# Attention heads: score banks, maxima banks, and the way the row sums leave PSUM

## The reference

```python
B, S, D, H = (4, 512, 512, 16)
DH = D // H
b, s, d = x.shape            # here b = 1, s = 2048, d = 512
q = (x @ Wq.T + bq).reshape(b, s, h, dh)
k = (x @ Wk.T + bk).reshape(b, s, h, dh)
v = (x @ Wv.T + bv).reshape(b, s, h, dh)
q = q * jnp.cos(rot)
k = k * jnp.sin(rot)
scores = jnp.einsum('bshd,bthd->bhst', q, k) / np.sqrt(dh)
scores = scores * spiral_weight[None, :, None, None]
attn = jax.nn.softmax(scores, axis=-1)
out = jnp.einsum('bhst,bthd->bshd', attn, v).reshape(b, s, d)
```

## Time and profile before

| | |
|---|---|
| median of 3 runs | 5249.96 us (5248.42 to 5251.48) |
| the profiled execution's span | 5264.5 us |
| PE, busy share of the span | 4694.6 us, 89% |
| DVE, ACT, POOL busy | 2373.3, 1652.7, 1662.5 us |
| the attention heads' stage | 1283 to 2275 us of the span |

### The profile page before, as it was taken

The page is one execution under the profiler, slowest core; times in us unless marked ns, Lnnn a source line. Parts: engine busy times, 40 slices in busy tenths (PEclk is TensorE's granted clock), DMA queues, the critical chain, the costliest instruction groups (busy, mean ns, idle before and its releaser), DMA issues. The chain is left out here.

```text
span 5264.5 us, 65210 instructions
## 1 busy us (share of the span) xinstructions
PE 4694.6 (89%) x25716; PEld 2520.4 (48%) x25716; DVE 2373.3 (45%) x3161; ACT 1652.7 (31%) x2791; POOL 1662.5 (32%) x1050
## 2 busy tenths in 40 slices
PE   7357997899999999986999869999999989789996
PEld 3123443433333333244666536666666654456663
DVE  7863778366666666853222223333333331412222
ACT  5414553211555555733111122222222210221111
POOL 1010000101888888023555401111111110145553
PEclk9678998999999999997999979999999999889998
DMA  2000000100000000016889730000000022468887
GB/s 72 0 2 19 6 0 8 60 0 1 1 1 1 1 1 1 1 68 184 253 260 259 169 119 23 31 31 31 23 31 31 23 81 80 157 173 257 256 257 200
DMA packets 237579, 417.60 MB, mean 79 GB/s; under 512 B 31472, under 2 KB 119536, under 8 KB 237296
## 3 DMA queue, kind: packets, MB, share of 16 engines
q1 hardware_dynamic: 179952, 270.89, 15.3%
q0 software_dynamic: 57344, 142.64, 11.1%
HBM read 297.53 MB, written 115.93 MB: 79 GB/s over the span
## 5 line engine op out<-in xcount | busy, mean ns | idle before, releaser
L2296 PE MATMUL linb_pr_ps<-lin_z,linb_wt 128*128 128x512 f32 x1536 | 678.9, 595 | 17.0 <-POOL linb_slope_own L2266 17.0
L1467 ACT ACTIVATE attc_prob<-attc_ps 128x512 f32<-128x512 f32 x1024 | 549.0, 596 | 426.6 <-PE attc_ps L1380 376.2
L1343 POOL TENSOR_TENSOR attc_acc<-attc_acc,attc_prob 128x2048 f32<-128x2048 f32 x144 | 651.4, 4524 | 68.0 <-ACT attc_prob L1467 49.9
L1491 DVE TENSOR_REDUCE attc_peak<-attc_ps 128x2 f32<-128x1024 f32 x384 | 469.6, 1225 | 256.1 <-PE attc_ps L1388 256.1
L1380 PE MATMUL attc_ps<-att_q,att_k 32*128 32x512 f32 x2048 | 527.7, 613 | 0.0
L2296 PEld LDWEIGHTS linb_pr_ps<-lin_z,linb_wt 128*128 128x128 f32 x1536 | 286.7, 192 | 343.3 <-issue 325.8
L1388 PE MATMUL attc_ps<-att_k,att_q 32*128 32x512 f32 x1536 | 442.3, 652 | 3.2 <-DVE attc_tot L1514 3.2
L2273 POOL TENSOR_TENSOR linb_sq<-linb_osb 128x512 f32<-128x512 f32 x64 | 70.1, 1096 | 1041.0 <-ACT linb_osb L2399 1041.0
L2472 DVE SCALAR_TENSOR_TENSOR linb_gated<-linb_osb,linb_norm_w,linb_proj 128x512 f32<-128x512 f32 x64 | 93.3, 1458 | 669.1 <-ACT linb_osb L2399 669.1
L1401 PE MATMUL attc_ps<-attc_prob,att_v 128*32 128x256 f32 (+1 forms) x3472 | 317.7, 438 | 0.3 <-ACT attc_prob L1467 0.3
L1023 DVE TENSOR_TENSOR_SCAN ssmb_state<-ssmb_decay,ssmb_bu 128x2048 f32<-128x2048 f32 x64 | 279.7, 4409 | 79.0 <-ACT ssmb_decay L970 79.0
(11 more groups left out here) (443 smaller groups left out, 7539.6 us busy)
## 6 DMA issues: line engine op xcount, KB each, us to landing
moe1w_wgu<-in_L_ffn_gate_up_proj SPq DMA_DIRECT2D x32, 1536.0 KB
moe2w_wgu<-in_L_ffn_gate_up_proj SPq DMA_DIRECT2D x32, 1536.0 KB
moe1w_wd<-in_L_ffn_down_proj SPq DMA_DIRECT2D x32, 512.0 KB
gated_features<-linb_gated SPq DMA_DIRECT2D x64, 256.0 KB
moe2w_wd<-in_L_ffn_down_proj SPq DMA_DIRECT2D x32, 512.0 KB
linc_gt<-gated_features SPq DMA_DIRECT2D x7, 2048.0 KB, 8.2
linb_wt<-in_L_attn_b_qkv_w SPq DMA_DIRECT2D x16, 768.0 KB
residual_rows<-residual SPq DMA_DIRECT2D x8, 1024.0 KB, 4.3
```

The lines of the kernel that those rows point to most:

```text
L1343: pool.tensor_tensor(acc[:, n % 2, :, :], before, prob[:, U % NP, :, :], ALU.add).then_inc(pool_done, 2 if at == 1 else 1)
L1467: nc.scalar.activation(prob[:, U % NP, h, :], ps[:, n % 3 if at < 0 else at % 6, :], ACT.Exp).then_inc(exp_done, 1)
L1491: V.tensor_reduce(peak[:, w // TT % 2, i % QH, 2 * hp:2 * hp + 2, b], ps[:, bank:bank + 2, :], axis=AX.X, op=ALU.max).then_inc(mx_used, 1)
L2296: last = nc.tensor.matmul(pr_ps[:, use % 2, :], wt[:, b, kind, k, :], z[:, k, t * NB:(t + 1) * NB], start=(k == 0), stop=(k == DT - 1))
```

## The change

Scores in groups 0 to 2 get four banks (0 to 3) in place of three. The uses get single banks, three of them in turn (4 to 6): each head's maximum is a use of its own, with its own wait, its own semaphore increment and its own reduction on DVE, and a use waits for the use three before it. The sums leave PSUM by a copy on ACT into `tot` (two buffers, semaphore `z_out`), and DVE inverts them there in four pieces of 128 columns, one in each of the units 2 to 5 of a block, and multiplies in unit 6. The accumulator of a block becomes two, for units 0 to 6 and 7 to 13 (HALF = 7), in a ring of three; POOL makes 12 adds instead of 13 a block, and `sums` has four sources instead of three.

```diff
+        HALF = 7
         SUMMED = (14, 15)
         POOLED = [i for i in range(TT) if i not in SUMMED]
         prob = L.sb("prob", [P, NP, QH, NB])
-        acc = L.sb("acc", [P, 2, QH, NB])
-        tot = L.sb("tot", [P, NB])
+        acc = L.sb("acc", [P, 3, QH, NB])
+        tot = L.sb("tot", [P, 2, NB])
         o_raw = L.sb("o_raw", [P, 2, NB])
...
-            got = ["A", "B"] if f < DT - 1 else []
-            if U >= LAG:
-                done = (U - LAG) % TT
-                if done == TT - 1:
-                    got.append("F")
-            if w % TT == 2 and ((f < DT - 1 and w > TT) or (f > 0 and w == 2)):
-                got.append("R")
+            got = [("peak", h) for h in (2, 3, 0, 1)] if f < DT - 1 else []
+            if U >= LAG and (U - LAG) % TT == TT - 1:
+                got.append(("sums", 0))
+            if w % TT == 2 and ((f < DT - 1 and w > TT) or (0 < f < DT and w == 2)):
+                got.append(("rows", 0))
             return got
 
-        use_at, n_use = {}, 0
+        LAST_GROUP = (DT - 1) * UNITS
+        use_at, sums_upto, others_upto = {}, [0], [0]
         for U in range(ALL + LAG):
-            for kind in uses_of(U):
-                use_at[U, kind] = n_use
-                n_use += 1
-        LAST_GROUP = (DT - 1) * UNITS
-        USES_BEFORE = min(n for (U, kind), n in use_at.items() if U >= LAST_GROUP)
-
-        def use_banks(U, kind):
-            if U >= LAST_GROUP:
-                return 6
-            return 3 + 2 * (use_at[U, kind] % 2)
+            for use in uses_of(U):
+                use_at[U, use] = len(sums_upto) - 1
+                sums_upto.append(sums_upto[-1] + (use[0] == "sums"))
+                others_upto.append(others_upto[-1] + (use[0] != "sums"))
+        USES_BEFORE = min(n for (U, use), n in use_at.items() if U >= LAST_GROUP)
+
+        def use_bank(U, use):
+            return 6 if U >= LAST_GROUP else 4 + use_at[U, use] % 3
+
+        def use_count(U, use):
+
+            return others_upto[use_at[U, use] + 1]
 
         def rows_block(U):
             f, w = U // UNITS, U % UNITS
             return (f * TC + w // TT - 1) if w > TT else (f * TC - 1)
+
+        def accumulator(n, half):
+            return acc[:, (2 * n + half) % 3, :, :]
...
                 for at, i in enumerate(POOLED):
-                    if at == 0:
+                    if at % HALF == 0:
                         continue
                     U = n * TT + i
                     pool.wait_ge(exp_done, (U + 1) * QH)
                     if at == 1 and n >= 2:
                         pool.wait_ge(z_done, n - 1)
-                    if at >= 2:
+                    if at == HALF + 1 and n >= 1:
+                        pool.wait_ge(z_done, n)
+                    if at % HALF >= 2:
                         pool.wait_ge(pool_done, n * len(POOLED) + at)
-                    before = prob[:, (U - 1) % NP, :, :] if at == 1 else acc[:, n % 2, :, :]
-                    pool.tensor_tensor(acc[:, n % 2, :, :], before, prob[:, U % NP, :, :], ALU.add).then_inc(pool_done, 2 if at == 1 else 1)
+                    to = accumulator(n, at // HALF)
+                    before = prob[:, (U - 1) % NP, :, :] if at % HALF == 1 else to
+                    pool.tensor_tensor(to, before, prob[:, U % NP, :, :], ALU.add).then_inc(pool_done, 2 if at % HALF == 1 else 1)
...
-            def take(U, kind):
-                n = use_at[U, kind]
-                if U >= LAST_GROUP:
-                    pe.wait_ge(mx_used, n)
-                elif n >= 2:
-                    pe.wait_ge(mx_used, n - 1)
-                return use_banks(U, kind)
+            def take(U, use):
+                n = use_at[U, use]
+                before = n if U >= LAST_GROUP else max(n - 2, 0)
+                if others_upto[before]:
+                    pe.wait_ge(mx_used, others_upto[before])
+                if sums_upto[before]:
+                    pe.wait_ge(z_out, sums_upto[before])
+                return use_bank(U, use)
 
             def score_bank(n):
-                if n < QH * LAST_GROUP:
-                    if n >= 3:
-                        pe.wait_ge(exp_done, n - 2)
-                    return n % 3
                 at = n - QH * LAST_GROUP
-                if at < 3:
-                    pe.wait_ge(exp_done, n - 2)
-                elif at < 6:
-                    pe.wait_ge(mx_used, USES_BEFORE)
+                if at < 4:
+                    if n >= 4:
+                        pe.wait_ge(exp_done, n - 3)
+                    return n % 4
+                if at < 6:
+                    pe.wait_ge(mx_used, others_upto[USES_BEFORE])
+                    pe.wait_ge(z_out, sums_upto[USES_BEFORE])
...
-            def maxima(U, kind, heads):
+            def maxima(U, heads):
                 f, w = U // UNITS + 1, U % UNITS
                 i, b = w // TC, w % TC
-                bank = take(U, kind)
                 for h in heads:
+                    bank = take(U, ("peak", h))
                     own = slice(h * DH, (h + 1) * DH)
-                    last = nc.tensor.matmul(ps[:, bank + h % 2, :], q[own, f, i * P:(i + 1) * P], k[own, f, b * NB:(b + 1) * NB],
-                                            start=True, stop=True)
-                last.then_inc(mx_done, 1)
+                    nc.tensor.matmul(ps[:, bank, :], q[own, f, i * P:(i + 1) * P], k[own, f, b * NB:(b + 1) * NB],
+                                     start=True, stop=True).then_inc(mx_done, 1)
...
-                sources = [prob[:, (n - 1) % NP, :, :], prob[:, n % NP, :, :], acc[:, n // TT % 2, :, :]]
+                sources = [prob[:, (n - 1) % NP, :, :], prob[:, n % NP, :, :], accumulator(n // TT, 0), accumulator(n // TT, 1)]
...
-                    maxima(U, "A", (2, 3))
+                    maxima(U, (2, 3))
                     if U >= LAG and (U - LAG) % TT:
                         values(U - LAG, 0)
                     scores(U, (2, 3))
-                    maxima(U, "B", (0, 1))
+                    maxima(U, (0, 1))
...
                 nc.scalar.copy(o_raw[:, n % 2, :], o_bank).then_inc(o_out, 1)
+                act.wait_ge(z_done, n + 1)
+                nc.scalar.copy(tot[:, n % 2, :], ps[:, use_bank(n * TT + TT - 1 + LAG, ("sums", 0)), :]).then_inc(z_out, 1)
...
-            def sums_out(U, kind):
-                n = (U - LAG) // TT
-                bank = use_banks(U, kind)
-                dve.wait_ge(z_done, n + 1)
-                V.reciprocal(tot[:, :], ps[:, bank, :]).then_inc(mx_used, 1)
-                dve.wait_ge(mx_used, use_at[U, "F"] + 1)
-                dve.wait_ge(o_out, n + 1)
-                f, t = n // TC, n % TC
-                V.tensor_tensor(q[:, f, t * NB:(t + 1) * NB], o_raw[:, n % 2, :], tot[:, :], ALU.mult).then_inc(o_used, 1)
+            def divide(n, step):
+
+                if step < QH:
+                    dve.wait_ge(z_out, n + 1)
+                    part = tot[:, n % 2, step * P:(step + 1) * P]
+                    V.reciprocal(part, part).then_inc(inverted, 1)
+                else:
+                    dve.wait_ge(inverted, QH * (n + 1))
+                    dve.wait_ge(o_out, n + 1)
+                    f, t = n // TC, n % TC
+                    V.tensor_tensor(q[:, f, t * NB:(t + 1) * NB], o_raw[:, n % 2, :], tot[:, n % 2, :], ALU.mult).then_inc(o_used, 1)
...
+            for U in range(ALL + LAG + QH + 1):
+                if LAST_GROUP <= U < ALL and U % TT in POOLED and POOLED.index(U % TT) % HALF:
                     add(U)
-                for kind in uses_of(U):
-                    if kind == "A":
-                        peaks(U, "A", 1)
-                    elif kind == "B":
-                        peaks(U, "B", 0)
-                        if U % TT == TT - 1:
-                            split(U)
-                    elif kind == "R":
+                for kind, h in uses_of(U):
+                    if kind == "peak":
+                        peak_of(U, h)
+                    elif kind == "rows":
                         rows_out(U)
-                    else:
-                        sums_out(U, kind)
+                if U < LAST_GROUP and U % TT == TT - 1:
+                    split(U)
+                since = U - LAG - TT
+                if since >= 0 and since % TT <= QH and since // TT < ALL // TT:
+                    divide(since // TT, since % TT)
```

More of the change, by code:

```diff
@@ L1404, in values, with sums @@
                     last.then_inc(pv_done, 1)
-            def sums(U, kind):
+            def sums(U):
                 n = U - LAG
-                bank = take(U, kind)
+                bank = take(U, ("sums", 0))
                 sem, count = summed_by(n - n % TT + POOLED[-1])
                 pe.wait_ge(sem, count)
-                sources = [prob[:, (n - 1) % NP, :, :], prob[:, n % NP, :, :], acc[:, n // TT % 2, :, :]]
+                sources = [prob[:, (n - 1) % NP, :, :], prob[:, n % NP, :, :], accumulator(n // TT, 0), accumulator(n // TT, 1)]
```

(57 more changed lines are left out.)

11 lines of the change are left out of this document (5 added, 6 removed).

## The result

The changed kernel takes 5273.32 us (median of 4 runs, 5272.69 to 5275.17) against 5249.19 us for the kernel before (4 runs, 5244.18 to 5251.48): the ratio is 1.0048, with a 95% interval of 1.0035 to 1.006. That is 24 us slower, where I had forecast 19 us faster, and outside my range.

A forecast was written before the change was run, and what follows sets the result against it. PE was taken to set the pace, with POOL close behind. Gains of 52.2 us less costs of 33.3 left 18.9 us, taken off the median of 5249.96: 5231 us, range 5204 to 5256.

The forecast's parts named there:

- The multiply (0.69) fits the gap: On DVE in the block: the multiply of 0.69 us was to fit between other work, with no cost charged.
- The fall of the clock: At nine block ends PE's clock falls; all nine were taken as gone, 1.53 us each, 13.8 us gained.
- rival B: The clock still falls in the long unit at block ends, so 13.8 us stay: 5245 us, chance 0.14.
- The same in `split`: DVE at a block's end: the split of 1.48 us delays the next reduction by 0.69, 11 times, 7.6 us lost.
- I took the stage's gain off the median: Whole program: the stage's 18.9 us gain was subtracted from the median, 5249.96 us, giving 5231 us.
- POOL's waits at a block's end: ACT's two waits for POOL, 0.74 and 0.90 us, both go: 18.8 us gained.
- The unit after the multiply's old place: At a block's end the reciprocal's wait goes: the last maximum is released 1.40 us earlier, 11 times, 15.4 us gained.
- The last group's entry: Where the last group begins, PE's standstills of 1.36 us for POOL and 2.83 for the reciprocal go: 4.2 us gained.
- The ring of three: Inside blocks the second maximum waits for an earlier reduction: units of 3.79 us, 0.03 more each, 5.0 us lost.
- rival A: The maxima's ring does not bind: a unit comes to 3.62 us, 29 us less, 5203 us, chance 0.12.
- Rivals C and D: C: DVE's loop dearer, 5256 us at 0.15 more a unit, chance 0.17. D: handover 0.05 more, 5240 us, chance 0.12.
- The quarters: DVE's reciprocal pieces of 0.95 us delay reductions in units of a block: 0.55 us, 11 times, 6.0 us lost.

The follow-up runs named there:

- e2: The changed kernel with the multiply moved from unit 6's place to step 14, where POOL has no add: 5237.38 us, ratio 0.9978.
- e5: As e2, with `split` also moved into unit 0 of the next block, where POOL pauses: 5227.06 us, ratio 0.9964.
- e9: The changed kernel with 72 more instructions of met waits ahead of PE's loop in the linear attention: 5256.61 us, ratio 1.0015.
- e8: The kernel before with 184 more instructions of met waits ahead of PE's loop in the linear attention: 5274.4 us, ratio 1.0055.
- e1: The kernel before, unchanged, run again for a second profile: 5245.75 us, ratio 0.9996.
- e12: As e5, with one accumulator for a block in place of the two halves: 5266.96 us, ratio 1.0037.
- e6: As e5, with PE waiting before a use on one semaphore in place of two: 5205.44 us, ratio 0.9921.
- e3_pad72: The changed kernel with 72 more waits, met at once, ahead of PE's program of the attention heads: 5247.42 us, ratio 0.9999.

## Why the prediction was wrong

Three steps failed. The first and the last were each worth as much as the whole forecast or more, the second 7 us.

**"The multiply (0.69) fits the gap"** was priced at nothing. It measured 37.4 us: eleven times a multiply of 2.9 us, the wait of PE behind it, and the clock's fall; moving it alone gave 38.6 back (e2). The length 0.69 was that of the kernel before, where the multiply runs at 1635.69, between two adds of POOL (one ends at 1634.75, the next starts at 1636.50), and I carried it to a place where POOL adds. The fall of the clock that I took as gone (13.8 us) did go from its place, as forecast, but for one; it came back in unit 7, in nine of eleven blocks. So rival B had its sign right and its place wrong.

**The same in `split`.** I charged 0.69 us a block, from 1.48 us read as its own length. About half of that was the cast waiting for POOL: it took 0.96 us and ended at 1622.50, 0.06 after an add of POOL, where the cast alone takes 0.20. In the new order it waits longer, and the unit takes 4.8 to 5.1 in ten blocks and 6.4 in one, where the clock falls too: 14.7 us for 7.6. Without POOL beside it, it costs nothing (e5).

**The rest of the program.** I took the stage's gain off the median, with all else unchanged. The change made PE's program longer, and the linear attention lost 18 to 22 us by its place (e9 against the changed kernel, and e8 against e1): stalls at the turns of its loop, and the clock's falls behind them.

The other terms stood. POOL's waits at a block's end went, by the two halves (e12). The unit after the multiply's old place gave 4.49 and 7.17 us for 4.5 and 7.2. The sums cost 0.86 a block. The last group's entry went from 45.45 us for block 12 to 41.56, 0.86 of dearer sums included, for 4.2 forecast. The ring of three was cheaper: a unit is 3.73 and not 3.79, about 10 us in all. Timeline of PE in the changed kernel, one unit, beside the earlier trace rows:

```profile
1603.15 0.39 PE L1385 MATMUL attc_ps<-att_rows,attc_ones 32*128 32x512 bf16 x2
...
1604.90 0.39 PE L1385 MATMUL attc_ps<-att_rows,attc_ones 32*128 32x512 bf16 x2
...
1606.88 0.39 PE L1385 MATMUL attc_ps<-att_rows,attc_ones 32*128 32x512 bf16 x2
```

The halves are 1.75 and 1.98: the ring binds in only one of them, which is rival A in part. Rivals C and D fall, since both made the unit longer. The quarters cost 0.14 us a block for 0.55, some 4.5 us less. Together: 37.4 + 7.1 - 10 - 4.5 = 30 us worse than forecast, where the heads' stage came out 25.2 worse (+6.3 for -18.9). Of the 5 between, 3.3 are the stage's first three units, 11.32 us for 14.63, which I had not counted.

The change alone, with the code at its old place, is thus slower by about 0.15% (e9), and with its two DVE operations at a better place and one wait in place of two it is 0.8% faster (e6, at about that place).

## What to carry to other kernels

An operation's duration belongs to its neighbours too: when it moves, ask which other engine will be working on SBUF at the new time, and read a duration in both surroundings before it is used as a price. Behind a ring without slack, one late instruction can cost more than its own length: here 2.1 us for the wait, and with the clock's fall behind it up to 4. And a change that lengthens an engine's program may move a loop in a later stage; look at that stage's "issue" waits and at the instruction queue before the change itself is blamed.

## What the runs showed of the hardware

Two small DVE instructions wait for POOL's add in progress. The multiply, with two inputs in SBUF, took 2.94 and 2.97 us beside adds and 0.68 without. The cast of 128 x 16 took 0.20 us alone, 1.33 to 1.36 beside an add that ended 0.05 to 0.07 us before it, and 3.96 in e12_one_accumulator (add's end 1621.60, cast's end 1621.67). Reductions from PSUM and quarters with one SBUF input kept their lengths beside the same adds. The add that started after the multiply took 4.77 us in place of 4.52.

The Trainium skill, page "SBUF — State Buffer", section "Who interferes with whom", states this: a DVE instruction with two SBUF inputs contends with a GpSimd instruction that reads SBUF, copies and casts can contend too, and the one that comes second is blocked until the other has ended. The trace agrees, with the numbers above. It is the rule that should have been weighed in the prediction.

The code of a loop of 1785 PE instructions (1784 from turn to turn in the trace) was loaded once or in every one of its seven turns, depending on where it began. The difference is 53 or 54 packets of 16 KB, six or twelve stalls of about 2 us, and 18 or 36 us of the stage (1198, 1216, 1234). Of the 35 us between the changed kernel and e3_pad72, 22 are the stalls and 13 a longer busy time of PE, with the granted clock at 0.50 behind the stalls.
